# A conditioned transformer block on one core: setup joined to the embedding stage, and the last masks loaded ahead of attention's first tiles

## What is computed

```
# L0: adapter with a chosen expert, on all rows
hidden = gelu(x @ down_W.T + down_b)                      # 512 -> 128
hidden = hidden @ expert_W[domain].T + expert_b[domain]   # per sample, one of 16
x      = layernorm((hidden + domain_emb[domain]) @ up_W.T + up_b + x) * gamma + beta
# L1: adaptive layernorm from the time step, attention, feed-forward
emb    = silu(sin_emb(timestep)) @ W_ada + b_ada          # 1024 = scale, shift
x      = ln(x) * (1 + scale) + shift
q,k,v  = x @ Wq + bq, x @ Wk + bk, x @ Wv + bv            # 16 heads of 32
probs  = softmax(where(mask, -inf, q k^T / sqrt(32) + bias))  # bias: 2 x 16 x 2048 x 2048
x      = x + (probs v) @ Wo + bo ;  x = x + ffn(ln(x))
# L2: rotation of groups of four columns by the angles theta and phi
# L3: a correction from the 32-column bases U, V after Gram-Schmidt, with a gate
```

## Time and profile before

| | |
|---|---|
| median of 3 runs | 3694.97 us (3692.91 to 3696.57) |
| profiled execution, its own time | 3693.57 us |
| its span in the records | 3691.8 us |
| mean granted TensorE clock | 0.987 of full speed |
| busy: PE, DVE, ACT, POOL | 97%, 61%, 59%, 56% |
| instructions | 79,762 |

### The profile page before, as it was taken

The page is one execution under the profiler, slowest core; times in us unless marked ns, Lnnn a source line. Parts: engine busy times, 40 slices in busy tenths (PEclk is TensorE's granted clock), DMA queues, the critical chain, the costliest instruction groups (busy, mean ns, idle before and its releaser), DMA issues. The chain is left out here.

```text
span 3691.8 us, 79762 instructions
## 1 busy us (share of the span) xinstructions
PE 3577.2 (97%) x32011; PEld 2457.6 (67%) x32011; DVE 2268.0 (61%) x4518; ACT 2178.7 (59%) x3038; POOL 2057.4 (56%) x778
## 2 busy tenths in 40 slices
PE   4999979999999999999999999999899999999999
PEld 2444448888888888888888888888444444444444
DVE  6766738888888888888888888888211111111112
ACT  1334338999989999989999899999111110210110
POOL 0111128999889898888999899987310110110100
PEclk8999989999999999999999999999999999999999
DMA  4455479999999999999999999998400100110102
GB/s 148 162 184 211 178 291 336 323 330 323 324 351 335 328 328 327 343 357 321 321 320 323 381 327 328 326 322 285 157 23 12 35 24 11 52 51 12 46 23 91
DMA packets 209550, 827.81 MB, mean 224 GB/s; under 512 B 24992, under 2 KB 58912, under 8 KB 133920
## 3 DMA queue, kind: packets, MB, share of 16 engines
q1 hardware_dynamic: 204832, 814.32, 63.7%
q10 hardware_dynamic: 4352, 8.39, 0.6%
HBM read 731.40 MB, written 91.23 MB: 223 GB/s over the span
## 5 line engine op out<-in xcount | busy, mean ns | idle before, releaser
L1137 POOL TENSOR_TENSOR at_tiles<-at_tiles,at_negmask 128x1792 f32<-128x1792 f32 x509 | 1827.4, 3634 | 243.5 <-DMA at_tiles<-in_bias 205.4
L1227 ACT ACTIVATE at_tiles<-at_tiles,at_rmin 128x2048 f32<-128x2048 f32 x512 | 1025.3, 2002 | 56.1 <-DVE at_rmin L1274 56.0
L1173 PE MATMUL at_ps_p<-consts,at_tiles 128*128 128x128 f32 x8192 | 1028.4, 273 | 0.1
L1173 PEld LDWEIGHTS at_ps_p<-consts,at_tiles 128*128 128x128 f32 x8192 | 934.6, 142 | 36.9 <-issue 0.4
L1235 ACT ACTIVATE at_prob_t<-at_ps_p 128x512 f32<-128x512 f32 x1536 | 830.6, 596 | 152.0 <-PE at_ps_p L1173 151.9
L1274 DVE CUSTOM_DVE_ANT_0 at_tiles<-at_ps_s,at_tiles 128x1024 f32<-128x1024 f32 x512 | 624.8, 1220 | 132.9 <-PE at_ps_s L1154 124.4
L1154 PE MATMUL at_ps_s<-at_k_stack,at_q_stack 128*128 128x512 f32 x2048 | 681.4, 434 | 18.5 <-DMA at_k_stack<-k_lo 13.2
L1274 DVE CUSTOM_DVE_ANT_0 at_tiles<-at_ps_s,at_tiles,at_rmin 128x1024 f32<-128x1024 f32 x512 | 657.8, 1285 | 19.1 <-PE at_ps_s L1160 0.9
L1190 PE MATMUL at_ps_c<-at_prob_t,at_v 128*32 128x128 f32 x16384 | 500.5, 274 | 0.6 <-DVE at_ctx_rows L1292 0.6
L1190 PEld LDWEIGHTS at_ps_c<-at_prob_t,at_v 128*32 128x32 f32 x16384 | 431.7, 110 | 43.8 <-issue 43.0
L1521 PE MATMUL ff_ps_m<-ff_norm_t,ff_w 128*128 128x512 f32 x1024 | 445.1, 595 | 0.5 <-ACT ff_feats L1660 0.5
(11 more groups left out here) (189 smaller groups left out, 2607.8 us busy)
## 6 DMA issues: line engine op xcount, KB each, us to landing
at_tiles<-in_bias SPq DMA_DIRECT2D x512, 1024.0 KB, 9.5
at_k_stack<-k_hi SPq DMA_DIRECT2D x128, 256.0 KB, 7.3
at_k_stack<-k_lo SPq DMA_DIRECT2D x128, 256.0 KB, 9.1
negm<-em_mask_out SPq DMA_DIRECT2D x32, 512.0 KB, 6.5
at_q_stack<-q_hi SPq DMA_DIRECT2D x128, 128.0 KB, 7.9
at_q_stack<-q_lo SPq DMA_DIRECT2D x128, 128.0 KB, 9.0
at_v<-v SPq DMA_DIRECT2D x64, 256.0 KB, 11.4
at_negmask<-negm SPq DMA_DIRECT2D x32, 512.0 KB, 13.6
```

Of the source, the lines that this page charges most:

```text
L1137: pool.tensor_tensor(tiles[s][:, 0:PCOLS], tiles[s][:, 0:PCOLS], negm[s][:, 0:PCOLS], ALU.add).then_inc(s_pool, 1)
L1173: last = pe.transpose(ps_p[k][:, y * P:(y + 1) * P], tiles[s][:, t * P:(t + 1) * P], ident)
L1227: act.activation(tiles[s][:, :], tiles[s][:, :], ACT.Exp, bias=rmin[:, s, 1:2], scale=-1.0, accum_out=rsum[:, s:s + 1]).then_inc(s_exp, 1)
```

## The change

1. The setup block is gone. Its work moves into the embedding block, and each engine waits for just the loads that it needs (`s_const`, `s_int`, `s_tab`, `s_dn`, `s_gsw`, `s_upw`, `s_wada`, `s_qw`, `s_kw`, `s_vw`).
2. The loads are issued in another order, on two queues: SP has constants, x, down, experts, up, U, V, up_b, gamma, beta, W_ada, Wq, Wk, Wv; ScalarE's queue has the time step, domain, angles, expert tables and b_ada (eight columns of 128 elements).
3. VectorE begins with sample 0's expert weights and the angles; sample 1's expert weights come at the end of round 0. The 16 experts are summed in two halves, in which each operation waits only for the one before the last (`pipelined`).
4. Scale and shift are made as columns: 32 matmuls with W_ada as the stationary side and the silu's two columns as the moving side. They are transposed back to 16 rows, stored, and loaded again as broadcast rows by SP in round 1 (the feed-forward part uses the rows).
5. The rotation rows and the bf16 identity are made in the last round.
6. SP loads the masks of each tile ahead of `load_attention_start`.

```diff
+    def pipelined(self, ins):
+        self.n += 1
+        ins.then_inc(self.sem, 1)
+        self.eng.wait_ge(self.sem, self.base + self.n - 1)
...
-            pe.wait_ge(s_w, 16 * n_w)
+            pe.wait_ge(s_const, 16)
...
             for r in range(NT + 1):
...
+                if r >= 1:
+                    after(sp, s_mk, MPR * p)
+                    sp.dma_start(mask_in[:], mask_v[p]).then_inc(s_mk_in, 16)
+                if r == 1:
+                    spread_ada_rows()
                 if r == NT:
                     load_attention_start()
                 if r >= 1:
-                    after(sp, s_mk, MPR * p)
-                    sp.dma_start(mask_in[:], mask_v[p]).then_inc(s_mk_in, 16)
...
+            def spread_ada_rows():
+                sp.wait_ge(s_adrc, 1)
+                sp.dma_start(net.ada, ada_rows[:]).then_inc(s_ada_st, 16)
+                sp.wait_ge(s_ada_st, 16)
...
             def ada_columns():
-                for i in range(4):
-                    src = (net.ada_scale, net.ada_shift)[i % 2][:, i // 2, :]
+                pe.wait_ge(s_wada, 16)
+                pe.wait_ge(s_silu, 1)
+                for o in range(2 * DC):
                     for c in range(DC):
-                        o = DC * i + c
-                        last = pe.transpose(ps_q[0][:, o:o + P], src[:, c * P:(c + 1) * P], ident)
+                        last = pe.matmul(ps_q[0][:, o * B:(o + 1) * B], w_ada[:, c, o * P:(o + 1) * P],
+                                         sig[:, c * B:(c + 1) * B], start=(c == 0), stop=(c == DC - 1))
...
+                link.pipelined(v.tensor_scalar(wacc[:, 0, :], ident, valid[:, 1, b:b + 1], None, ALU.mult))
+                link.pipelined(v.tensor_scalar(wacc[:, 1, :], experts[:, 0, :], hotv[:, b, 0:1], None, ALU.mult))
+                for e in range(1, EXPERTS):
+                    half = wacc[:, (e + 1) % 2, :]
+                    link.pipelined(v.scalar_tensor_tensor(half, experts[:, e, :], hotv[:, b, e:e + 1], half, ALU.mult, ALU.add))
...
+            expert_weights(0)
+            angles()
             v.memset(ones[:], 1.0)
...
+            dve.wait_ge(s_gsw, 2 * 16)
             gs_products(gs[0], first)
-            add_up_bias(0, range(TJ))
             for r in range(NT + 1):
...
                     v.tensor_scalar(hid2[:], ps_d[:], net.exp_bias[:, batch_of(r):batch_of(r) + 1], None,
                                     ALU.add).then_inc(s_hid2, 1)
+                if r == 0:
+                    dve.wait_ge(s_upw, 4 * 16)
+                    add_up_bias(0, range(TJ))
...
                 if r == 0:
-                    dve.wait_ge(s_adt, 1)
-                    v.tensor_copy(ada_col[:], ps_q[0][:, 0:4 * DC]).then_inc(s_adc, 1)
+                    silu()
...
                     take_end(4)
+                    v.tensor_copy(net.ident_bf[:], ident)
+                    rotation_rows()
...
                     gs_project(r, 3)
+                if r == 0:
+                    take_ada_rows()
+                    expert_weights(1)
```

More of the change, by code:

```diff
@@ L92, in __call__ @@
         self.eng.wait_ge(self.sem, self.base + self.n)
[L97 to L236, removed]
-            for n in range(2 * B):
-                b, k = divmod(n, 2)
-                dve.wait_ge(s_ada, n + 1)
-                to = net.ada_scale[:, b, :] if k == 0 else net.ada_shift[:, b, :]
-                ins = v.tensor_tensor(to, ps_ada[n % 2][:], b_ada[:, k * D:(k + 1) * D], ALU.add)
-                ins.then_inc(s_ada_out, 1)
-                if k == 0:
-                    dve.wait_ge(s_ada_out, n + 1)
-                    link(v.tensor_scalar(to, to, 1.0, None, ALU.add))
-        @block.tensor
-        def _(pe):
-            pe.wait_ge(s_rep, 1)
-            pe.wait_ge(s_big, 5 * 16)
-            for n in range(2 * B):
-                b, k = divmod(n, 2)
-                after(pe, s_ada_out, n - 1)
-                for c in range(DC):
-                    last = pe.matmul(ps_ada[n % 2][:], rep[:, c, b, :], w_ada[:, c, k * D:(k + 1) * D],
-                                     start=(c == 0), stop=(c == DC - 1))
-                last.then_inc(s_ada, 1)
@@ L333, in embed_stage @@
         qk32 = sb("em_qk32", [P, 2, TOK])
+        with ExitStack() as early:
+            w_ada = early.enter_context(nc.sbuf_tensor("em_w_ada", [P, DC, 2 * D], F32))
+            experts = early.enter_context(nc.sbuf_tensor("em_experts", [P, EXPERTS, P], F32))
         qk_hi = sb("em_qk_hi", [P, 2, DC, TOK], F32R)
@@ L495, in project @@
                 g = 12 * p + i
+                if p == 0 and i in (0, 4, 8):
+                    pe.wait_ge(*((s_qw, 3 * 16), (s_kw, 16), (s_vw, 2 * 16))[i // 4])
                 if g == 0:
                     pe.wait_ge(s_adc, 1)
+                elif g == 1:
+                    pe.wait_ge(s_adrc, 1)
                 elif g >= 3:
@@ L660, in take_qk @@
                 act.wait_ge(s_qk, 8 * p + i + 1)
+                if p == 0 and i == 0:
+                    act.wait_ge(s_qw, 3 * 16)
                 after(act, s_split, 8 * p + i - 1)
@@ L1859, in build_program @@
         net.v = scratch("v", [B * S // TJ, TJ * D])
+        net.ada = scratch("ada", [4 * D * B // (2 * P), P])
         net.negm = scratch("negm", [B * S, S], BF16)
```

191 lines of the change are left out of this document (169 added, 22 removed).

## The result

The changed kernel takes **3672.75 us** (median of 5 runs, 3664.73 to 3681.44), the kernel before 3694.97 (5 runs, 3691.99 to 3700.26). The ratio is 0.9936, with an interval of 0.9918 to 0.9954: some 22 us faster. The forecast was 3655.0 with a range of 3647 to 3668. So the sign was right, and the gain about half of the 40.1 us of the sum. The profiled execution of the changed kernel took 3671.38 us, with a span of 3669.3; against the one of before, 3693.57, that is 22.2 us less.

A forecast was written before the change was run, and what follows sets the result against it. TensorE (busy 97%) was taken as the bound except at the start and in a late hole. Gains of 24.2 and 15.9, together 40.1, from 3693.57 give 3653.5; with 1.4 for the median, 3655, range 3647 to 3668.

The forecast's parts named there:

- the two places: Where TensorE was not the bound: the start, until round 1, and a hole from 489 to 503 us.
- The tail: Last masks' load ahead of attention's loads: TensorE gets back a wait of 14.2 and slow matmuls' 1.7, together 15.9 us.
- Rival A: Last round: the hole only moves, to later masks, tail stores or a DMA backlog; 3669 if all 14.2 returns; chance 0.12.
- Step 1: Start, loads: the expert weights and small loads that VectorE waits for land by 12 us (bounds 11.0 and 34.5).
- rival D: VectorE's first wait: small loads starve; landing at 34.5 gives 3677; chance 0.05 short of its turning point, 0.03 past it.
- Step 2: VectorE, sample 0's expert weights: two halves overlap, operations 0.27 us apart, 4.6 us in all, ready at 19.1.
- Rival B: Expert weights on VectorE: the two halves bring nothing, 6.5 us in place of 4.6, 1.9 later, 3657; chance 0.12.
- Steps 3 and 4: VectorE, start: angles, first Gram-Schmidt products, then the bias on x; first add 29.0 us ahead, first residual 27.9 ahead.
- Step 5: TensorE, round 0: 64 column instructions behind up projection (ends near 32) take 9.5 us; 3.5 lost (0 to 10), 24.4 ahead.
- Rival C: Scale and shift columns on TensorE: all 64 at 0.24 and a late start, 10 lost not 3.5, 3662; chance 0.12.
- Step 7: Round 1: VectorE gets the row copy and sample 1's expert weights, 7.0 us where it idled 5.79; nothing lost.

The follow-up runs named there:

- experiment 1: Only the last masks' load moved ahead of attention's loads, on the kernel before: 3681.68 us, ratio 0.996.
- experiment 2: The changed kernel with the masks' load put back behind attention's loads, leaving the new start alone: 3686.57 us, ratio 0.9965.
- experiment 8: The reordered start of experiment 5, with attention's third tile issued behind the stores of q and of masks 0 and 1: 3653.67 us, ratio 0.9878.
- Experiment 5: The changed kernel with second dots ahead of the 64-instruction group, silu right behind the bias on x, and angles ahead of expert weights: 3648.14 us, ratio 0.9864.
- Experiment 3: The changed kernel with the 64 two-column instructions put behind the second Gram-Schmidt dots on TensorE: 3666.23 us, ratio 0.9895.
- experiment 6: The changed kernel with silu alone moved, right behind the bias on x, the group still ahead of the dots: 3664.86 us, ratio 0.9913.
- experiment 7: The changed kernel with each of the 64 two-column instructions done a second time: 3687.81 us, ratio 0.9973.

## Why the prediction was wrong, point by point

- **The bound, and the two places.** Right: the work of TensorE is unchanged and both gains came from idle time. Experiments 1 and 2 separate them, and they add.
- **The tail, 15.9.** Right: 16.0 in the two profiles, 15.5 to 16 and 16.7 of time in experiment 1. Masks 2 and 3 waited 6.50 us for the stores, as foreseen, and it cost TensorE nothing in this block; neither did the moved rotation rows. In attention it may have cost a little: some 15 us after its start TensorE waited 2.60 us where the kernel before had 0.21, and experiment 8, with earlier stores, cut such a wait from 3.42 to 1.06. But experiment 1, with the masks' load moved too, has 0.18 there, so the move alone doesn't bring it. Rival A (the hole only moves) is out, though its 3669 is the nearest to the time that was measured. A time that fits is no evidence for the mechanism.
- **Step 1, loads by 12.** 3.2 too early: the index came at 15.19. Beside the large loads the small ones took 8.7 and 11.7 us from issue to landing; I had one land every 1.3 us. That they waited for the large ones is argued, as no run takes these away. The Trainium skill (DMA: Bandwidth & Descriptors, Issuing engines are not separate DMA queues) has the queues interleave on the same 16 engines, and this trace agrees: the last table landed at 15.05, amid the large loads, and not at 34 with the last of them. So rival D did not come about, and one us of step 1 cost one us, as it had said. It reached the first residual (24.9 ahead in place of 27.9). Experiment 5 shows how to hide it.
- **Step 2, expert weights, 0.27 apart.** Right: 15 in 4.02 us, against 5.78 when each waited for the one before. Rival B is out. The Trainium skill (VectorE: DVE Perf Modes, The DRAIN you can't avoid) says that leaving the semaphores out saves nothing. Here two interleaved chains, with their semaphores, saved 1.8 of 5.8 us, and for them the measurement decides. The same section adds that a next operation which nothing holds starts earlier; that is nearer to what these runs show.
- **Steps 3 and 4.** Right but for the 3.0 that they inherit: angles and products took from 22.1 to 28.5, and the bias adds, now behind the first add, 3.3 from there to the residual, as written.
- **Step 5, the columns: the step that failed.** It said "Up projection ends near 32", a start there, 9.5 us, and 3.5 lost. Measured: a start at 41.08, 13.79 us, and a wait of 13.07. The start is the greater part, 9.1 of the 13.4 by which the two terms miss: 5.6 of it is TensorE's wait for silu, and 3.4 is that the up projection itself ended only at 35.4, most of this for the late loads. I had looked at what the group waits for on TensorE's own queue, and not at its other operand. Silu is a VectorE multiplication, and VectorE's program has it behind the round's moments. So the chain became: moments, silu, TensorE's group, dots, VectorE. VectorE waited on TensorE, which had waited on VectorE for an operand that nobody else wanted, and whose inputs were there from 29 us on. The other 4.3 is the length: the whole group ran at 1.2 GHz, at 0.215 each, and not just a first stretch of it. VectorE in turn asked for the dots at 42.4, not at 38.4 (3.0 for the loads, 1.0 for a slower up projection), so of the 13.5 us by which they were late it saw 9.6 as more wait. Experiment 3 takes the place away (13.4 us earlier), 6 the late silu (10.8), 7 doubles the length (13.6 later). Rival C named the low clock and a late start, but sized them at 10 in all.
- **Step 7, round 1.** Right: the dots ask without a wait, and 10.7 of 10.9 is still there.
- **The sum.** 40.1 had 24.2 for the start, and 10.7 was measured: 13.5 missing, 3.0 of it the loads (they would have cost that without the group too) and 10.5 step 5. To the 26.7 that was left, attention added 1.2 (TensorE waited 2.4 less for the stacks of k and 2.4 more for VectorE at the start, and its work took 1.5 less), and 1.0 went in the feed-forward part. Then 4.4 went at the end, where the profile of before was the unusual one. 26.7 + 1.2 - 1.0 - 4.4 = 22.5, which is the difference of the spans.
- **The range** (3647 to 3668) failed with step 5: I priced "0 to 10 lost" there, from the length alone, and no bound held a start later than the queue's own. The late loads alone would not have done it: 3672.75 less step 5's 10.5 lies inside the range, and less the loads' 3.0 it doesn't.

Two things stay open. Attention's length, 2061.9 to 2072.4 us over these profiles, follows no change of mine in a way that I could show. And why the clock fell later in the one profile of before is open.

## What to carry to other kernels

When work moves to an engine that seems free, list all operands of its first instruction with the place at which each is issued on its own engine, and then who stands behind it. A group put "in a gap" that waits for one late operand holds everything queued behind it, and it may then run at another clock than it would have had directly behind the work before it. Three moves of a line or two (the dots ahead of the group, silu as soon as its inputs are there, the angles into the wait for the tables) took the kernel from 3673 to 3648 us, or from 25.2 to 51.6 under the kernel before.

## What the runs showed of the hardware

- **VectorE beside GpSimd.** In the last round of after one split took 3.95 us and the bf16 identity 3.40, where the same operations take 0.69 and 0.21 (0.21 in experiment 8). Both lie within GpSimd's three adds of 480.73 to 492.02, and each ends at about the end of one of them: 480.73 + 2 x 3.76 = 488.3 against 488.57, and 492.02 against 492.10. In experiment 8 no add ran beside the identity, and it was short; in experiment 7 the identity (0.22) ended as the adds began at 499.36, and two operations on the rotation rows behind it took 3.67 each, where experiment 8 has 0.27. Before, VectorE had nothing to do while those adds ran, since the hole lay there. The Trainium skill (SBUF — State Buffer, Who interferes with whom) says that the two share a pair of ports which one instruction holds until it ends; this trace agrees. It cost nothing here, as TensorE had 13.9 us of v projection to do.
- **The clock of the group, and its price.** In after and in experiments 3, 5 and 7 TensorE had waited 2.35 to 5.64 us right ahead of the group or of the dots before it; the clock was at 0.50 for all of the group, and an instruction took 0.214 to 0.215. In experiment 6, with no wait ahead of it, the clock was full for the first 5.4 us and then fell while TensorE went on without a pause. So idle time ahead of the group is not all that brought the clock down, and what else did isn't settled; nor did it rise again in the 27 us of experiment 7. At 0.214 each, the 3.4 us at the low clock in experiment 6 hold 16 instructions, which leaves 48 for 5.4 us: an estimate of 0.11 each at the full one. Two columns are thus hardly cheaper than 128: 16 transposes had taken 1.91 at the full clock, 0.12 each. The weight loads of the group in after were busy for 13.73 of its 13.79 us.
- **An issue can hold its queue for long.** The eight issues of 0.5 KB of em_b_ada kept ScalarE's queue for 7.61 us. That small loads are the reason isn't shown: in the same stretch the one issue of em_up, 256 KB, kept SyncE's for 7.32.
